# Delta-rule front stage: beta from 64 small TensorE products, norms by a ScalarE root and a VectorE reciprocal, query scaling on GpSimd, 16x16 blocks inverted by columns

## What is computed

```
x = layernorm(x)
q = l2norm(split(x @ Wq)); k = l2norm(split(x @ Wk)); v = split(x @ Wv)   # 4 heads of width 32
beta = sigmoid(x @ Wbeta)                                                # one number per token and head
for t in tokens:                        # state S, 32 x 32 for each batch and head
    err = (v_t - k_t @ S) * beta_t
    S   = S + outer(k_t, err)
    o_t = q_t @ S
```

## Time and profile before

| | |
|---|---|
| profiled execution | 2025.36 us |
| its span | 2023.6 us |
| `delta_front`, start to the last inverse | 0 to 123.1 us |
| in it: busy DVE / POOL / PE / ACT | 106.59 / 82.61 / 57.80 / 49.56 us |
| mean granted TensorE clock in it | 0.80 of full |
| `delta_solve` | to about 190 us |
| `delta_scan` | to about 260 us |
| the other layers | to 2023.6 us |

### The profile page before, as it was taken

One profiled execution on the slowest core, in us unless ns is written; L12 is line 12 of the kernel. 1 busy time (PEld: TensorE's weight loads), 2 busy tenths in 40 slices (PEclk: granted clock), 3 DMA queues, 4 the chain that ended last, 5 costly groups with the idle time before them and its releaser, 6 DMA issues. The chain is left out here.

```text
span 2023.6 us, 49215 instructions
## 1 busy us (share of the span) xinstructions
PE 1781.0 (88%) x18950; PEld 823.9 (41%) x18950; DVE 1626.9 (80%) x3052; ACT 1291.7 (64%) x2719; POOL 1135.7 (56%) x712
## 2 busy tenths in 40 slices
PE   6538857999999955968999999999999999999997
PEld 3337832233333344654433344434444343444334
DVE  7942567999999475438778999999999999999963
ACT  5403243888888710217866677777877777777785
POOL 8723541000000055331136888999999999989995
PEclk9768976899999956989998999999999999999998
DMA  1220045111111061137993323323232323233211
GB/s 48 36 50 3 1 147 191 42 48 42 46 48 39 13 201 52 48 96 265 386 386 87 83 67 82 80 69 82 68 85 64 85 66 83 72 77 77 73 28 42
DMA packets 194493, 180.22 MB, mean 89 GB/s; under 512 B 58740, under 2 KB 155124, under 8 KB 194052
## 3 DMA queue, kind: packets, MB, share of 16 engines
q1 hardware_dynamic: 185860, 170.01, 28.9%
q0 software_dynamic: 2944, 7.10, 1.1%
q10 hardware_dynamic: 5504, 0.73, 0.2%
HBM read 101.16 MB, written 75.26 MB: 87 GB/s over the span
## 5 line engine op out<-in xcount | busy, mean ns | idle before, releaser
L977 DVE TENSOR_REDUCE maxima_l<-max_l 128x1 f32<-128x512 f32 x1024 | 652.0, 678 | 46.5 <-PE max_l L1087 40.2
L953 POOL TENSOR_TENSOR part_sums_l<-probs_l 128x1024 f32<-128x1024 f32 x256 | 615.2, 2403 | 98.2 <-ACT probs_l L1043 85.4
L1043 ACT ACTIVATE probs_l<-exp_l 128x512 f32<-128x512 f32 x1024 | 568.1, 598 | 139.5 <-PE exp_l L1098 135.2
L1087 PE MATMUL max_l<-k_stack_l,q_stack_l 96*128 96x512 f16 x1024 | 399.3, 391 | 4.2 <-DVE pv_bank_l L969 3.3
L1098 PE MATMUL exp_l<-q_stack_l,k_stack_l 100*128 100x512 f16 x1024 | 389.6, 381 | 2.5 <-ACT probs_l L1043 1.6
L1305 DVE TENSOR_REDUCE maxima_l<-max_l 128x1 f32<-128x512 f32 x512 | 317.0, 682 | 17.0 <-PE max_l L1391 16.8
L1342 ACT ACTIVATE probs_l<-exp_l 128x512 f32<-128x512 f32 x512 | 279.3, 599 | 58.5 <-PE exp_l L1404 54.8
L1132 PE MATMUL pv_bank_l<-probs_l,v_ring_l 128*32 128x512 f32 x2048 | 273.6, 606 | 0.3 <-issue 0.3
L1819 POOL IOTA rows_e<- 128x32 int32 x1 | 0.2, 184 | 386.5 <-POOLq L26 386.5
L1087 PEld LDWEIGHTS max_l<-k_stack_l,q_stack_l 96*128 96x128 f16 x1024 | 100.0, 98 | 280.7 <-DVE maxima_l L977 189.8
L984 DVE TENSOR_TENSOR part_sums_l<-part_sums_l 128x512 f32<-128x512 f32 x128 | 182.3, 1424 | 14.4 <-POOL part_sums_l L953 14.3
(11 more groups left out here) (297 smaller groups left out, 2563.1 us busy)
## 6 DMA issues: line engine op xcount, KB each, us to landing
scratch_qk_l<-parts_g SPq DMA_DIRECT2D x128, 256.0 KB, 9.2
q_stack_l<-scratch_qk_l SPq DMA_DIRECT2D x192, 128.0 KB
k_stack_l<-scratch_qk_l SPq DMA_DIRECT2D x192, 128.0 KB
scratch_v_l<-v_g SPq DMA_DIRECT2D x16, 1024.0 KB
v_ring_l<-scratch_v_l SPq DMA_DIRECT2D x64, 256.0 KB, 3.3
scratch_stack_l<-parts_c SPq DMA_DIRECT2D x16, 384.0 KB, 3.6
q_stack_l<-scratch_stack_l SPq DMA_DIRECT2D x64, 96.0 KB, 2.2
k_stack_l<-scratch_stack_l SPq DMA_DIRECT2D x64, 96.0 KB, 2.3
```

Source lines behind the costliest of these rows:

```text
L953: pool.tensor_tensor(part_sums[:, i, h, :, :], probs[:, i, h, 0:2, :], probs[:, i, h, 2:4, :], ALU.add).then_inc(pair_sum.sem, 1)
L977: dve.reduce_max(maxima[:, s % 2, at % NT, at // NT:at // NT + 1], max_bank(n, at)[:, :], AX).then_inc(max_taken.sem, 1)
L1043: act.activation(probs[:, i, at // NT, at % NT, :], exp_ps[at % 2][:, :], ACT.Exp, scale=a.scale).then_inc(prob_tile.sem, 1)
L1087: pe.matmul(max_bank(n, at)[:, :], qs[0:SHIFT_ROW, s % RING, h, k * P:(k + 1) * P], ks[0:SHIFT_ROW, s % RING, h, :], start=True, stop=True ...
```

## The change

The diff, cut to its core:

```diff
+            def scale_queries(b):
+                q = raw[:, b % 2, 0, :, :]
+                pool.wait_ge(inv_norm_ready.sem, inv_norm_ready.made(b, 0))
+                pool.tensor_tensor(q, q, bc(inv_norm[:, b % 2, 0, :], DA), ALU.mult).then_inc(q_normed.sem, 1)
...
             for i in range(B + 3):
                 if i >= 3:
                     mask_keys(i - 3)
-                if i < B:
-                    pool.wait_ge(norm2_ready.sem, norm2_ready.made(i, 0))
-                    if i >= 2:
-                        pool.wait_ge(normed.sem, normed.made(i - 2, 1))
-                    pool.tensor_tensor(inv_norm[:, i % 2, :, :], norm2[:, i % 2, :, :],
-                                       g.minus_half[:, 0:2 * CH].rearrange("p (s c) -> p s c", s=2), ALU.pow).then_inc(inv_norm_ready.sem, 1)
+                if 1 <= i < B + 1:
+                    scale_queries(i - 1)
...
-                dve.wait_ge(proj_ps.sem, proj_ps.made(b, 2))
-                if b >= 1:
-                    dve.wait_ge(beta_exp.sem, beta_exp.made(b - 1, 0))
-                dve.transpose(beta_rows[:, :, :], by_chunk(beta_bank)).then_inc(beta_raw.sem, 1)
...
+            def invert_norms(b):
+                dve.wait_ge(norm_ready.sem, norm_ready.made(b, 0))
+                dve.reciprocal(inv_norm[:, b % 2, :, :], norm[:, b % 2, :, :]).then_inc(inv_norm_ready.sem, 1)
+
             def normalise(b):
...
-                dve.tensor_tensor(q, q, bc(inv_norm[:, b % 2, 0, :], DA), ALU.mult).then_inc(normed.sem, 1)
...
-            def invert(half, rows):
+            def invert(half, columns):
                 batches = slice(half * B // 2, (half + 1) * B // 2)
-                for i in rows:
-                    if i == 1:
+                for j in columns:
+                    if j == 0:
                         dve.wait_ge(a_loaded[half], 16 * (B // 2))
-                    for_j = a_blocks[:, batches, i, 0:i].unsqueeze(2).broadcast_to([P, B // 2, i, i])
-                    did(dve.tensor_tensor(terms[:, :, 0:i, 0:i], for_j, inv[:, batches, 0:i, 0:i], ALU.mult))
+                    wide, low = j + 1, LB - 1 - j
+                    a_column = a_blocks[:, batches, wide:LB, j].unsqueeze(2).broadcast_to([P, B // 2, wide, low])
+                    row = bc(inv[:, batches, 0:wide, j], low)
+                    did(dve.tensor_tensor(terms[:, :, 0:wide, wide:LB], row, a_column, ALU.mult))
                     settle()
-                    row = dve.tensor_reduce(inv[:, batches, 0:i, i], terms[:, :, 0:i, 0:i], AX, ALU.add, negate=True)
+                    below = inv[:, batches, 0:wide, wide:LB]
+                    rest = dve.tensor_tensor(below, below, terms[:, :, 0:wide, wide:LB], ALU.subtract)
...
             for i in range(B + 1):
+                if i >= 1:
+                    invert_norms(i - 1)
                 if i < B:
                     to_tokens(i)
...
-                act.wait_ge(beta_raw.sem, beta_raw.made(b, 0))
-                act.activation(g.beta[:, b, :], beta_rows[:, :, 0], ACT.Exp, scale=-1.0).then_inc(beta_exp.sem, 1)
+                act.wait_ge(proj_ps.sem, proj_ps.made(b, 2))
+                act.activation(g.beta[:, b, :], beta_bank[:, 0:CH], ACT.Exp, scale=-1.0).then_inc(beta_exp.sem, 1)
+
+            def roots(b):
+                act.wait_ge(norm2_ready.sem, norm2_ready.made(b, 0))
+                if b >= 2:
+                    act.wait_ge(inv_norm_ready.sem, inv_norm_ready.made(b - 2, 0))
+                act.activation(norm[:, b % 2, :, :], norm2[:, b % 2, :, :], ACT.Sqrt).then_inc(norm_ready.sem, 1)
...
                 if i == 3:
                     act.wait_ge(zeroed, 1)
+                if i < B:
+                    roots(i)
                 if i >= 3:
                     cross(i - 3)
...
+                for c in range(CH):
+                    for h in range(HA):
+                        last = pe.matmul(beta_bank[h * DA:(h + 1) * DA, c:c + 1], xnT[:, b % 2, c * DA:(c + 1) * DA], w_beta[:, h:h + 1],
+                                         start=True, stop=True)
+                last.then_inc(proj_ps.sem, 1)
```

53 lines of the change are left out of this document (25 added, 28 removed).

## The result

The kernel with the change takes **2047.27 us** (median; 2044.94 to 2064.89), the kernel before, run beside it, 2024.61 us (2024.28 to 2027.73). The ratio is 1.0124, with a 95% interval of 1.0081 to 1.0167. So it is slower, by 22.7 us, where 10.0 were forecast; the interval of the ratio reaches from 16 to 34 us, and the median lies just above the end of the forecast's range, 2047. The profiled execution took 2047.54 us, its span is 2045.8 us.

The account below looks back on a forecast made before the run. GpSimd's bound on the loop was to pass to a ring through ScalarE: 8.8 us to the mask, less 5.6 in the tail, plus 6.8 for the clock, +10.0 on 2025.36, median 0.8 lower: 2034.6 us; range 2024 to 2047.

Parts of the forecast that it names:

- the ring through ScalarE: Front loop: squares, root, cross copies, centring, xnT copy, q and back to squares; period 10.7 us at full clock.
- The squares of batch 7: ScalarE in the front loop: start at 84.8 us at full clock, against 72.86 before.
- Beta's 128 records: TensorE in each batch: the 64 small products for beta take 2.0 us, ends 1.5 and 3.6.
- I cost them at nothing: ScalarE's two table loads per batch, 1.28 us each, are covered by the wait for the sums; uncovered, 2.6 us a batch.
- rival 3: ScalarE: table loads cost double through a drain, 7 times 1.75 = +12 us, total about 2041; chance 0.07.
- To the mask of batch 5: Front, from batch 7's squares through root, copies, GpSimd and q's transposition: mask at 95.5 us, 8.8 later than before.
- The tail: Front's end, mask of batch 5 to last inverse: 30.7 us in place of 36.3, giving back 5.6.
- SyncE's chain from the mask to the last load's issue takes 16.9 us: Tail: with 2.3 us landing, it keeps half 1 from beginning before mask + 19.2 us.
- 1.04 ns per element: VectorE's inversion steps in the tail: about 0.16 us plus this rate, giving 11.5 us per half by columns.
- the clock's term of 6.8: TensorE in the front loop: clock falls in 4 of 7 batches, 1.7 us each, +6.8 us.
- Everything behind the stage is unchanged: After the front: no cost, except a table load in delta_scan that lies off its chain.
- The closing remark that left code fetching out: TensorE: twice the instructions, but code fetching as idle reason left out since no such wait stands on the ring.

Follow-up runs that it names:

- the idle products: Changed kernel plus seven 128x128 identity products per batch in TensorE's queue, read by nothing, to hold its clock up: 2034.02 us, ratio 1.0050.
- padded kernel: Kernel before plus 504 tiny unread products in TensorE's queue at the end of the front: 2029.62 us, ratio 1.0031; run again, 2049.19 us.
- late root, split stores: Changed kernel with beta as before, root behind the next batch's xnT copy, ScalarE issuing half the stores of the last two batches: 2025.25 us, ratio 0.9996.
- the late root: Changed kernel with ScalarE's root behind the next batch's xnT copy and VectorE's reciprocal behind the next sums: 2029.66 us, on another chip 2050.56.

## Why the prediction was wrong in size

Right was the kind: GpSimd falls out as the bound, and the ring through ScalarE takes over because the root stands ahead of cross copies, centring and xnT. By steps, with what each was worth:

- **The squares of batch 7** were forecast at 84.8 at full clock and 6.8 later with four falls of the clock, 91.6. They came at 92.67. That this is so near is luck, since two errors nearly cancel. Beta's 128 records took 1.24 us at full clock, not 2.0 (below the lower bound of 1.5), so the period at full clock is shorter than 10.7: it was 10.2 where the idle products held the clock up (57.07 to 67.24). And the clock was low in five of seven q products and partly low in a sixth, not in four. Holding it up from batch 4 on took 6.6 us off this point (86.08).
- **"I cost them at nothing"**, the table loads, was nearly right, though its cover of 0.8 us (4.74 against 3.96) was gone: with cheaper beta products the sums come as early as the second load ends. The loads held up the root by 1.36 us in batch 3 and by 0.07 or less elsewhere. Without loads the last inverse comes 3.4 us earlier, with the clock low in other batches. The double price of rival 3 wasn't seen: activations follow a load within 0.02 us.
- **To the mask of batch 5** 10.7 us were forecast, 12.9 were measured (92.67 to 105.55). The root came 5.33 us behind the squares of batch 7 instead of 4.92. The copies of batch 5's products then ended at 100.86, but GpSimd began to mask them (`qk_d`) only at 102.17: the mask of beta (`beta_mask`, 101.16 to 102.21) stands ahead in its order and had waited for VectorE's mask of batch 4 (100.39). The forecast has no such step; it took 1.3 us. And `qk_d` took 1.71 us instead of 1.26.
- **The tail** was forecast at 30.7 us and took 34.9 (105.55 to 140.40), the largest miss in the front. The step "SyncE's chain from the mask to the last load's issue takes 16.9 us" was taken from before as if the masks were ready when SyncE was. In fact half 0 waited 2.7 us for a load behind the stores of batch 4, the mask of batch 6 stands in VectorE's order behind five columns of that half, and SyncE stood idle until it came (111.71 to 113.57): 19.0 us to the last issue. Half 1 was costed at 1.04 ns per element for every operation and took 13.1 us instead of 11.5, because of the column's stride.

Together: 1.0 + 2.2 + 4.2 = 7.4 us more in the front, which is 17.4 instead of 10.0. Holding the clock up from batch 4 on took 7.8 us off the front (140.40 - 132.59), and q was still at low clock in batches 1 to 3, so the clock's term of 6.8 was too small rather than too large. (Rival 3 is 2040 by its own terms, not 2041.)

- **"Everything behind the stage is unchanged"** was wrong as a cost of nothing. The profiled execution lost another 4.8 us there: 1.0 in solve, 0.8 in scan, 3.0 behind. The padded kernel, whose front ended 2.6 us late, was 4.0 us slower, and taking beta out of the change gave back about 7 us, of which 2.7 in the front. So a part of the 4.8 may belong to the 2,000 added instructions, but no run shows it: the distance from the last inverse to the end of the span scatters from 1893.6 to 1906.1 us over the profiles without the stop, the change being at 1905.4 and the highest a kernel without them (late root, split stores). The closing remark that left code fetching out looked for it on the ring, where it costs little, and not in the loops behind, where it can cost 20.

Of the change's parts the runs show this: columns are a gain of 4 us. The norms by root are a loss of 16.5, most of it by the root's place (4 to 8 are left with the late root). Beta is a loss of 1 to 7 by the company it stands in, and 4.0 come with as many idle products too. The stretch behind the front stays open but for the stop.

## What to carry to other kernels

An engine that works in written order shouldn't wait for a result of its own batch while work for the next batch stands behind: moving the root three calls down took 18 us off the front without removing an instruction. If TensorE gets onto such a ring, its clock can fall to half behind an idle gap, which makes the ring longer again (here q took 2.03 to 2.08 us behind gaps of 1.4 to 4.5 us, though once 1.12 behind 2.84); the price of a new wait is then found with the clock in it. A product that is replaced by 64 small ones should be counted in instructions too, since these can be paid far behind, in loops that didn't change (20 to 24 us of solve here).

## What the runs showed of the hardware

- 128 records with a 128x32 stationary side and one moving column take 1.24 us at full clock, 9.7 ns each, and 1.89 at low clock, which is less than twice.
- Idle products of TensorE that wait for nothing come in groups of 128 records with "issue" between them: in the padded kernel from 102 us on 1.88 us of work at the low clock, then 1.85 to 2.4 us of "issue". With the weight loads that is 256 instructions in 3.7 to 4.3 us. The Trainium skill (Runtime: NRT & Kernel Launch, Instruction fetch mechanics) says that instructions come in blocks of 16 KiB, 256 of them, and that TensorE's memory holds 2048. The size of the groups agrees. It also calls that memory a FIFO, refilled block by block. Here the loop of solve, 768 records and as many weight loads, has stalls of up to 2.5 us in its first pass and of at most 0.9 in the next ones, as if its code were kept from pass to pass. Only behind the stop does it stall as in the first. What the stop is no run here shows.
- A pass of 128x256 fp32 on VectorE whose operand is read with a stride of 64 bytes takes 0.59 us, with neighbouring elements 0.43.
- An `ACT_TABLE_LOAD` takes 1.28 us, and the next activation begins 0.01 to 0.02 us behind it, in all pairs of the change's loop that don't wait for data.
